# One product of a recurrent layer moved from GpSimd to VectorE, and the weight loads put in another order

## What is computed

```python
xn = layernorm(x)                                   # x: 2 x 16384 x 1024, float32
B = xn @ W2 + b2;  C = xn @ W3 + b3                 # 16 columns each
delta = softplus(xn @ W1 + b1)                      # 1024 columns
y = einsum('bln,bldn->bld', C, xn[..., None] * einsum('bld,bln->bldn', delta, B))
xq = quantize_rows_to_4_bits(xn @ H)                # H: Hadamard matrix over sqrt(1024)
wq = ternary(weight)                                # -1, 0, 1 times a scale for each row
out = x + y * silu(xq @ wq.T)
```

## Time and profile before

| | us |
|---|---|
| median of 3 runs | 539.49 (539.48 to 540.78) |
| the profiled execution | 539.21 |
| its span on the slowest core | 537.7 (others 534.7 to 537.5) |
| busy PE / DVE / ACT / POOL | 342.3 / 308.9 / 344.5 / 324.7 |

### The profile page before, as it was taken

The page is one execution under the profiler, slowest core; times in us unless marked ns, Lnnn a source line. Parts: engine busy times, 40 slices in busy tenths (PEclk is TensorE's granted clock), DMA queues, the critical chain, the costliest instruction groups (busy, mean ns, idle before and its releaser), DMA issues.

```text
span 537.7 us, 7160 instructions; the slowest of 8 cores (534.7 to 537.7 us)
## 1 busy us (share of the span) xinstructions
PE 342.3 (64%) x1664; PEld 149.2 (28%) x1696; DVE 308.9 (57%) x600; ACT 344.5 (64%) x393; POOL 324.7 (60%) x215
## 2 busy tenths in 40 slices
PE   0000546399797877788778797877887879755200
PEld 0000232244343333333333333333333334322000
DVE  1780088455586676766667766667666664543210
ACT  1601053466979898778888888888888877664220
POOL 2021044012477777777777777777777777777773
PEclk9999957599898999989989898998989899896755
DMA  7749421325445554444555554444445234222010
GB/s 187 229 140 168 50 79 21 59 31 128 80 117 118 129 139 142 121 119 127 130 121 123 135 130 118 118 119 117 119 129 127 78 97 84 79 76 59 39 78 39
DMA packets 80973, 57.78 MB, mean 107 GB/s; under 512 B 70435, under 2 KB 70564, under 8 KB 80932
## 3 DMA queue, kind: packets, MB, share of 16 engines
q1 hardware_dynamic: 72916, 34.19, 29.5%
q0 software_dynamic: 8016, 23.14, 13.5%
HBM read 25.93 MB, written 16.78 MB: 79 GB/s over the span
## 4 chain that ended last, share of the span: by engine, by line
POOL 51%; DVE 16%; issue 13%; PE 8%; DMA 5%; ACT 2%; POOLq 1%; DVEq 1%; SPq 1%; ACTq 0%
POOL ob L33 14%; POOL t4b L33 14%; POOL t1b L33 12%; DVE t3b L33 7%; POOL uT L33 5%; POOL vT L33 5%; DMA W1c<-w 3%; DVE tbf L33 3%; DMA xb<-x 2%; PE psZ L270 2%; DVE absum L33 2%; PE psZ L271 2%; DVE cst L33 1%; PE psO L291 1%; PE psO L292 1%
## 5 line engine op out<-in xcount | busy, mean ns | idle before, releaser
L33 POOL TENSOR_TENSOR t4b<-t3b,o3s 128x1024 f32<-128x1024 f32 x32 | 75.3, 2352 | 67.9 <-DVE t3b L33 67.9
L270 PE MATMUL psZ<-W1c,xnT 128*128 128x512 bf16 x256 | 102.1, 399 | 3.4 <-DVE bcw L33 3.4
L291 PE MATMUL psO<-ternT,xqT 128*128 128x512 bf16 x255 | 99.0, 388 | 8.2 <-DMA xqT<-xqb 4.9
L292 PE MATMUL psO<-ternT,xqT 128*128 128x512 bf16 x256 | 99.2, 388 | 4.6 <-DMA xqT<-xqb 4.6
L271 PE MATMUL psZ<-W1c,xnT 128*128 128x512 bf16 x256 | 101.2, 396 | 0.0
L316 PE MATMUL psXH<-Hs,vT 128*128 128x512 bf16 x128 | 58.6, 458 | 52.6 <-ACT xqm L33 50.8
L33 DVE SCALAR_TENSOR_TENSOR t3b<-xnb,cc,t1b 128x1024 f32<-128x1024 bf16 x32 | 41.1, 1284 | 75.5 <-POOL t1b L33 75.3
L33 POOL TENSOR_TENSOR ob<-xb,t4b 128x1024 f32<-128x1024 f32 x32 | 75.3, 2354 | 4.6
L33 POOL TENSOR_TENSOR t1b<-del,s 128x1024 f32<-128x1024 bf16 x32 | 68.5, 2141 | 7.9 <-ACT s L33 4.1
L33 ACT ACTIVATE esb<-psO,nsa 128x1024 f32<-128x1024 f32 x32 | 35.7, 1116 | 51.2 <-DVE o3s L33 50.8
L33 POOL TENSOR_TENSOR uT<-xnT 128x512 bf16<-128x512 bf16 x32 | 38.2, 1194 | 38.1 <-DMA xnT<-xnb 37.3
(11 more groups left out here) (53 smaller groups left out, 545.4 us busy)
## 6 DMA issues: line engine op xcount, KB each, us to landing
xb<-x SPq DMA_DIRECT2D x32, 512.0 KB, 4.2
out<-ob POOLq DMA_DIRECT2D x32, 512.0 KB, 3.3
wfst<-wf POOLq DMA_DIRECT2D x8, 512.0 KB, 4.1
W1c<-w POOLq DMA_DIRECT2D x8, 256.0 KB, 9.0
Hs<-hpk SPq DMA_DIRECT2D x1, 512.0 KB
xnT<-xnb SPq DMA_TRANSPOSE x32, 3.0
xqT<-xqb SPq DMA_TRANSPOSE x32, 3.1
W23s<-w POOLq DMA_DIRECT2D x1, 64.0 KB, 3.5
```

What stands on the lines that cost most here:

```text
L33: inst = fn(*a, **kw)
L270: pe.matmul(psZ1[:, 0:512], lh, W1c[ic][:, 0:512], start=(ic == 0), stop=False)
L291: pe.matmul(ps[:, 0:512], lh, ternT[:, ic * DM:ic * DM + 512], start=(ic == 0), stop=(ic == KC - 1))
L292: last = pe.matmul(ps[:, 512:1024], lh, ternT[:, ic * DM + 512:(ic + 1) * DM], start=(ic == 0), stop=(ic == KC - 1))
```

## The change

It has three parts. t1b is computed on VectorE, directly before t3b, and no longer on GpSimd; the semaphore sPT1 isn't used any more. GpSimd's queue issues the loads of W1 first, then all of wf. VectorE's blocks of preparation move: in pass -1 they come at the end, after bcw and dot of the first tile, and not at the start of the pass, and one prep_pre and the prep_cp of later blocks shift to the next passes.

```diff
--- before.py
+++ after.py
@@ -206,11 +206,9 @@
                     g.wait_ge(sTBF, oc - 2)
                 g.dma_start(out=wfstage[oc % 3][:], in_=wf_hbm[oc * 128:(oc + 1) * 128, :]).then_inc(sWFa[oc % 3], 16)
 
-            for k in range(6):
-                wf_load(k)
             for ic in range(KC):
                 w1_load(ic)
-            for k in range(6, KC):
+            for k in range(KC):
                 wf_load(k)
             gs = Ser(g, sSELFG)
             for c in range(-4, nt + 4):
@@ -225,10 +223,6 @@
                                      ALU.subtract, _inc=(sUVT, tu + 1))
                 w2 = c - 4
                 if 0 <= w2 < nt:
-                    g.wait_ge(sSIG, w2 + 1)
-                    if w2 >= 1:
-                        g.wait_ge(sDT4, w2)
-                    gs.tensor_tensor(t1buf[:], delta[w2 % 6][:], s2[w2 % 3][:], ALU.mult, _inc=(sPT1, w2 + 1))
                     g.wait_ge(sDT4, w2 + 1)
                     g.wait_ge(sO3S, w2 + 1)
                     g.wait_ge(sLDa[w2 % 11], 16 * (w2 // 11 + 1))
@@ -393,13 +387,10 @@
                                             ALU.mult, _inc=(sTBF, oc + 1))
 
             for c in range(-4, nt + 4):
-                if c == -1:
-                    prep_pre([0]); prep_pre([1]); prep_cp([0]); prep_pre([2]); prep_cp([1])
-                    prep_pre([3]); prep_cp([2]); prep_pre([4])
                 if c == 0:
-                    prep_cp([3]); prep_pre([5]); prep_cp([4]); prep_pre([6]); prep_cp([5])
+                    prep_cp([2]); prep_pre([4]); prep_cp([3]); prep_pre([5]); prep_cp([4]); prep_pre([6])
                 if c == 1:
-                    prep_pre([7]); prep_cp([6]); prep_cp([7])
+                    prep_cp([5]); prep_pre([7]); prep_cp([6]); prep_cp([7])
                 u = c - 1
                 if 0 <= u < nt:
                     dv.wait_ge(sPEXH, u + 1)
@@ -439,11 +430,14 @@
                     dv.tensor_copy(o3s[w_ % 2][:], psO3x[w_ % 2][:], _inc=(sO3S, w_ + 1))
                 w2 = c - 4
                 if 0 <= w2 < nt:
-                    dv.wait_ge(sPT1, w2 + 1)
+                    dv.wait_ge(sSIG, w2 + 1)
+                    dv.tensor_tensor(t1buf[:], delta[w2 % 6][:], s2[w2 % 3][:], ALU.mult)
                     if w2 >= 1:
                         dv.wait_ge(sVOUT, w2)
                     dv.scalar_tensor_tensor(t3buf[:], xnbf[w2 % 8][:], cc[w2 % 4][:], t1buf[:],
                                             ALU.mult, ALU.mult, _inc=(sDT4, w2 + 1))
+                if c == -1:
+                    prep_pre([0]); prep_pre([1]); prep_cp([0]); prep_pre([2]); prep_cp([1]); prep_pre([3])
 
     return nc
```

## The result

| | before | after |
|---|---|---|
| median, us | 539.72 (539.22 to 541.72, 8 runs) | 513.83 (512.53 to 515.2, 8 runs) |
| ratio | | 0.9513, 95% interval 0.9495 to 0.9532 |
| span of the profiled run, slowest core | 537.7 | 513.7 (others 506.1 to 513.5) |
| from one t3b to the next in the loop | 12.71 | 11.95 |

The change takes away 25.9 us, 4.9%. The prediction had 513.0.

A forecast was written before the change was run, and what follows sets the result against it. GpSimd sets the pace, with VectorE, ScalarE and TensorE having only one to three microseconds to spare. From 539.2 us: -15.2 +1.0 -3.5 -3.7 -12.8 +8.2 = -26.0, giving 513; range 500 to 527, 8 in 10.

The forecast's parts named there:

- t1b on VectorE: Loop, tiles 4 to 23: t1b takes 1.22 us, period 11.95 instead of 12.71, 0.76 less per tile, -15.2 us.
- The clock: Loop: TensorE at half clock in XH makes bcw late; prod waits behind vT, six tiles of 20 lose 1.37, +8.2 us.
- The first loop tiles: Tiles 0 and 1: t3b of tile 0 has no slack and gets t1b in front, +1.0 us together (0 to +2.6).
- The start: Before the loop: W1 lands near 33, dot ends at 35, first mx at 82.5 instead of 95.3, -12.8 us.
- Tiles 24 to 26: After the x statistics: t1b, held by the port, comes behind vT; tiles of 11.55 us, 3 x -1.15 = -3.5 us.
- Tiles 27 to 31: Last tiles, no uT and vT: the 2.17 wait for t1b becomes 1.43, 5 x -0.74 = -3.7 us.
- (b): Rival, start: it gives nothing because W1, x and first transposes crowd each other; mx stays at 95, 526 us, 12%.
- (a): Rival, loop: TensorE's clock stays up once the pipe is denser, 505 us, 18%.
- (c): Rival, loop: late bcw becomes the rule, each of 20 tiles loses 1.37, +27.4 instead of +8.2, 532 us, 12%.
- (d): Rival, loop: slower; TensorE at half clock through XH and into W1's product in every tile, period 14.0, 546 us, 4%.
- (e): Rival, loop: t1b no faster on VectorE (2.14 us), period 12.87, 539 us, the move does nothing, 4%.

The follow-up runs named there:

- fill6: The changed kernel with six extra 512-column matmuls per tile, result unused, on TensorE between the small product and the wait for XH; 506.02 us, ratio 0.9358.
- start_only: The kernel before with only the start changed (W1's loads first, preparation behind the first bcw), t1b still on GpSimd; 529.2 us, ratio 0.9795.
- prod_psum: The changed kernel with prod reading its first factor from PSUM instead of the SBUF copy; 506.48 us, ratio 0.9365.
- hold4: The changed kernel with W1's second half and all wf loads held until the first transpose xnT has landed; 517.55 us, ratio 0.9574.

## Why the prediction was right, point by point

- **t1b on VectorE, 1.22 us, period 11.95**: right. The mean of 24 rows in the loop is 1.225, the distance 11.95. The move alone gave 15.3 in the time, long tiles included.
- **The clock, six long tiles of 1.37 (+8.2)**: the mechanism is right, and fill6 shows the cause; that the size is right too is in part luck. On the profiled core six tiles are longer by 1.29 to 1.63, together 8.1; on the others one to six are. But the prediction took six tiles at half clock instead of eight because the wait before XH would get 0.76 shorter. There were more of them, not fewer: on the profiled cores ten of the twenty XH of tiles 4 to 23 ran at half clock, all or in part, where it had been eight, and the granted clock in the loop was 0.92 where the earlier trace rows has 0.95. The wait before those XH had shrunk only to 1.98, from 2.19 to 2.36. Of the ten, six made a long tile, two made bcw late at a cost of 0.1 or less (prod between uT and vT), and in two, right behind the two odd tiles of the last section, bcw didn't wait at all. Two other XH behind the same wait of 1.98 (at 254.25 and 316.61) ran at full clock; what decides isn't shown. And two more tiles, on every core, are 1.29 longer for another reason that the prediction didn't have (last section): from the t3b of tile 3 to that of tile 23 the time fell by 4.6 us where -15.2 and +8.2 make -7.0.
- **The first loop tiles (+1.0)**: not there. From first mx to the t3b of tile 3 the time fell by 0.4.
- **The start (-12.8)**: mis-sized, 9.1. The step that failed is "lands at 32.3, say 33, and with 1.9 from landing to dot the end of dot is at 35". W1 landed by 33.7 as worked out, but the small product has a second input, xnT, and I gave its transpose no price with the loads of W1, wf and x in flight, though the earlier trace rows showed what such traffic does to xb, and the third transpose of that trace what it does to xnT (15.7 us). In the kernel before the xnT of the first tile had long landed when W1 came. So the end of dot is at 39.8, 4.8 later. From there to the first mx it took 46.3 where 47.5 were worked out, eight blocks at 4.95 us against 4.96.
- **Tiles 24 to 26 (-3.5)**: 5.1, nearer to the -6 that the prediction named for a t1b not held up by vT. t1b didn't come behind vT. It slipped in between uT and vT, and vT waited for it. GpSimd's timeline after, tile 24 to 25:

```profile
440.44 1.16 POOL L33 TENSOR_TENSOR uT<-xnT 128x512 bf16<-128x512 bf16 x1
441.74 1.97 POOL L33 TENSOR_TENSOR vT<-xnT 128x512 bf16<-128x512 bf16 x1
```

VectorE's at the same place:

```profile
441.28 1.41 DVE L33 TENSOR_TENSOR t1b<-del,s 128x1024 f32<-128x1024 bf16 x1
442.81 1.98 DVE L33 SCALAR_TENSOR_TENSOR t3b<-xnb,cc,t1b 128x1024 f32<-128x1024 bf16 x1
```

  t1b is asked for within uT and ends at 442.69, 1.09 behind uT; vT then takes 1.97 instead of 1.16. The tiles last 12.15, 10.07 and 10.76 us instead of 11.55. So the port wait works in both directions, and here t1b, which had asked before uT ended, came before vT, which follows uT by 0.14; the next tile shows the same (vT 1.97).
- **Tiles 27 to 31 (-3.7)**: 9.33 to 9.34 in three of them, as worked out (9.34), 10.05 in the first. The last took 7.47: no o3s stands in front of its t1b, which was asked for at 493.91 while t4b ran, waited for the port (2.81 instead of 1.23) and was done before ob, which took 3.14. Together -4.8.

On the profiled core the terms came to -9.1 (start), -0.4 (first tiles), -4.6 (tiles 4 to 23, clock included), -5.1 and -4.8, that is -24.0, the difference of the two spans, where the prediction had -26.0: a start that gave 3.7 less and two long tiles of 2.6 that nobody expected, against 1.4 in the first tiles and 2.7 in the last. The profiled execution of after is 515.3, 1.5 above its median, so the median lies 0.8 from 513.0: part of that closeness is luck, since a start that gave too little and two long tiles that nobody expected were in part made up by other terms.

The rivals: (b), the start gives nothing, fell (start_only 11.2), though it named what took 3.7 us of it, transfers crowding each other. (a) didn't happen by itself; fill6 makes it happen, and gives 506 where (a) said 505. (c) would have been a long tile every time, and the half clock made six. (d) asked for bcw later than 9.1 us behind the end of t3b; the latest in the loop started 8.6 behind it (366.50, after a t3b that ended at 357.90). (e) fell with the 1.23 of t1b.

## What to carry to other kernels

When an engine's line of work is shortened, look who has a microsecond or less to spare and at what clock TensorE stands after its waits: prod_psum gave 7 of the 13 to 19 us worked out for it, and the rest came only when TensorE was kept busy. A first load that is moved to the front of the queues is not the only thing its consumer needs; price every input of the first instruction with that traffic in flight, and look in the trace for a transfer of the same kind that already ran beside it. A tiny VectorE operation with two inputs in SBUF costs what is left of GpSimd's instruction beside it; let one of them be in PSUM if it comes from there.

## What was not expected

- **A transpose behind the loads**: 3.62 us with half of W1 and all of wf held back, 16.13 with all in flight (hold4 and after).
- **A gap of 0.3 us that becomes 1.3.** In the fifth and the 22nd distance from t3b to t3b every core has a long tile, with the filling matmuls too, and bcw doesn't wait for TensorE in it. VectorE after, the fifth:

```profile
190.58 0.15 DVE L33 TENSOR_SCALAR msq<-msq 128x1 f32<-128x1 f32 x1
191.04 0.16 DVE L33 SCALAR_TENSOR_TENSOR var<-ssq,msq 128x1 f32<-128x1 f32 x1 [0.30 <-DVE msq L33]
191.30 1.53 DVE L33 SCALAR_TENSOR_TENSOR nmrs<-mean,rs 128x1 f32<-128x1 f32 x1
```

  var starts 0.30 late, so nmrs, 128x1, asks while uT runs (191.64 to 192.80) and takes 1.53 instead of 0.16, and prod meets vT. With t1b on GpSimd such a gap costs nothing: in the kernel before bcw comes 0.37 late at 353.45, in a tile of 12.70, since VectorE waits 2.19 for t1b there in any case. Two such tiles cost 2.6 us, beside the 24.0 that this core gained. What makes the gap is not settled: no row shows it, and it wasn't tested.
- **A matrix engine that does more is faster**: 22 us more of busy TensorE in 260 us, and 7.8 us less in all.
